# Moving the stacked copies of the keys from SyncE's queue to ScalarE's in a two-layer graph attention kernel

## The chip, the cores and the metric

One Trainium2 chip; the kernel runs on one of its cores. The metric is the device time of one launch in microseconds. Three runs of the kernel before took 1937.61 us (median; 1935.70 to 1940.65).

## The reference

The input `x` is 32 batches of 256 nodes by 384 features, `adj` is 32 sparse 256x256 matrices. Three layers follow each other, all in fp32; the outer two normalisations have no learned scale.

```python
def graph_layer(h, adj, wl, bl, ws, bs, wr, br, g, beta):          # twice: layers a and b
    a     = softmax(h @ h.T / sqrt(384), axis=-1)
    delta = a * adj
    attn  = delta / (delta.sum(-1, keepdims=True) + 1e-10)
    hl, hs, hr = h @ wl.T + bl, h @ ws.T + bs, h @ wr.T + br
    ctx = (attn * upper) @ hl + diag(attn)[:, None] * hs + (attn * lower) @ hr
    return relu(layernorm(ctx, 1e-12) * g + beta)

y   = layernorm(x + graph_layer_b(graph_layer_a(x)))
q, k, v = heads(y @ Wq + bq), heads(y @ Wk + bk), heads(y @ Wv + bv)   # 12 heads of 32: layer c
s   = where(adj > 0, q @ k.T / sqrt(32) + 0.1 * adj, -9e15)
out = layernorm(y + softmax(s) @ v)
```

## The kernel before

A batch is two row tiles of 128 nodes. Every fp32 operand of a large product is held as a rounded high part and a low rest, and each product is three matmuls (high x high, low x high, high x low). ScalarE (ACT) writes the high part out of PSUM, VectorE (DVE) subtracts it to get the low one.

The kernel is a software pipeline over batches: in pass `t`, layer a works on batch `t`, layer b on batch `t-1`, attention (layer c) on batch `t-2`, and the last normalisation on batch `t-3`. Within a pass each engine has a fixed list of steps, written out in `ORDER` (L46 to L77). A word `scores.8-1` is step `scores`, part 8, of the pass before (`-1`: it belongs to the batch that entered attention one pass ago). The five lists run beside each other and meet only at semaphores, so where a step stands in its engine's list decides what it is queued behind. There is no dynamic scheduling.

Names used below, for one batch in attention:

- `q.g`, `k.g` (g = 0 to 2): projection of 128 of the 384 query or key features, on TensorE (PE) into `bank_w`; ACT writes `qk_hi` (L666), DVE `qk_lo` (L863). `v.i` (i = 0, 1): the values; ACT writes them at L674, DVE the rest at L872.
- `q_stack.r`, `k_stack.r` (r = 0 to 3): the copies that this document is about. Heads r, r+4 and r+8 lie in the partitions 32r to 32r+31 of `qk_hi` and `qk_lo`. Three DMAs, one per slot, put high, low and high (for keys high, high, low) of these three heads under each other in 96 partitions of `q_st` and `k_st` (32 partitions x 3 heads x 256 fp32, 96 KB each), so that one matmul over 96 rows gives the whole three-term product of a head. So a batch has 12 DMAs for the queries and 12 for the keys.
- `scores.n` (n = 0 to 11, heads in the order of `HEADS`, L41): two matmuls `bank_s<-k_st,q_st`. They wait for the query and key copies of their group r; `scores.0` needs group 0, `scores.3` group 1, `scores.6` group 2, `scores.9` group 3. DVE adds the mask and takes the minimum (L883), ACT takes the exponential (L682).
- `weights.n`: ACT (L690) and DVE (L888) write the two fp16 halves of the weights, then SyncE (SP) issues a DMA transpose of them into `pT` (L355). `attend.n` multiplies `pT` with the values into `bank_o`.
- `b_proj.0` to `b_proj.5`: the three projections of layer b for two row tiles, alternating between the two PSUM banks `bank_w0` and `bank_w1`. `b_proj.2` writes bank 0 again, and so waits until ACT (L611) and then DVE (L790) have read `b_proj.0` out of it; `b_proj.3` waits likewise for `b_proj.1`.

Both DMA transposes and the 24 copies, and the loads of `x` and `adj`, are issued by SP in its own order. ACT issues one store per batch (L658). The lines of the lists that matter here: after the three key projections PE does `k.2 turn_h.1 v.0 turn_h.2 attend.10-1 v.1 turn_x.0 attend.11-1 b_scores.0 turn_x.1 scores.0 b_proj.0 scores.1 b_proj.1 b_proj.2 b_proj.3`, and ACT does `turn_x.0 v.0 v.1 scores.0 b_proj.0 turn_x.1 weights.0 scores.1 b_proj.1`.

Of the kernel before, what the change touches and what calls it, by code (L numbers as in the profile page):

```python
# [21 lines left out]
F32 = mybir.dt.float32  # L22
# [11 lines left out]
SLOTS = 3  # L34
# [22 lines left out]
        turn_h.0 k.1 weights.11-1 turn_h.1 k.2 turn_h.2 turn_x.0 v.0 v.1 scores.0 b_proj.0 turn_x.1 weights.0  # L57
        scores.1 b_proj.1 b_scores.0 weights.1 b_proj.2 b_turn.0 turn_x.2 b_proj.3 scores.2 b_proj.4 weights.2
        c_norm.0 scores.3 b_proj.5 weights.3 a_scores.0 c_apply.0 c_store.0 scores.4 weights.4 b_norm.0
        a_proj.0 b_apply.0 scores.5 weights.5 a_proj.1 scores.6 weights.6 a_turn.0 a_proj.2 scores.7 a_proj.3  # L60
        b_norm2.0""",
# [12 lines left out]
        weights.5-1 k_stack.3-1 q_stack.3-1 weights.6-1 a_x.0 weights.7-1 c_adj.0 weights.8-1 weights.9-1  # L74
        weights.10-1 q_stack.0 weights.11-1 k_stack.0 k_stack.1 b_adj.0 weights.0 q_stack.1 k_stack.2 a_adj.0
        weights.1 b_x.0 weights.2 q_stack.2 weights.3 weights.4""",
# [35 lines left out]
def graph_attention_kernel(nc, x, adj, wl, ws, wr, bl, bs, br, ln_w, ln_b,  # L112
# [3 lines left out]
    NC = D // P  # L116
    HD = D // NH
    HPG = P // HD
# [9 lines left out]
    with ExitStack() as ctx:  # L128
# [42 lines left out]
        qk_hi = sb("qk_hi", [P, 2, NC, S], F32R)  # L171
        qk_lo = sb("qk_lo", [P, 2, NC, S], F32R)
        q_st = sb("q_st", [P, NH, S], F32R)
# [89 lines left out]
        def wait(eng, s, count):  # L263

            if count > 0:
                eng.wait_ge(s, count)
# [38 lines left out]
        def _(sp):  # L305
            def stack(t, side, r):

                c = t - 2
                if r == 0:
                    wait(sp, s_qk_lo, NC * (2 * c + side + 1))  # L310
                for slot in range(SLOTS):
                    part = (qk_hi, (qk_lo, qk_hi)[side], (qk_hi, qk_lo)[side])[slot]
                    sp.dma_start((q_st, k_st)[side][slot * HD:(slot + 1) * HD, r::HPG, :].bitcast(F32),  # L313
                                 part[r * HD:(r + 1) * HD, side, :, :].bitcast(F32)).then_inc(s_stack["qk"[side]][r], 16)
# [43 lines left out]
            def load(n):  # L358
# [9 lines left out]
                "q_stack": lambda t, r: stack(t, 0, r), "k_stack": lambda t, r: stack(t, 1, r),  # L368
# [183 lines left out]
        def _(act):  # L552
# [132 lines left out]
            def weights(t, k):  # L685
# [6 lines left out]

            steps = {
                "split": split, "turn_x": turn_x, "turn_h": turn_h, "turn_y": turn_y,
# [349 lines left out]
```

## Time and profile before

| | |
|---|---|
| median of three runs | 1937.61 us |
| profiled execution: its own time | 1934.71 us |
| profiled execution: span, first to last instruction | 1933.0 us |
| busy share PE / DVE / ACT / POOL | 91% / 80% / 65% / 34% |
| mean granted clock of TensorE | 0.976 of full speed |
| DMA queue of SP, of ACT: share of 16 engines' time | 57.2%, 2.1% |

The program has 36 passes, of which some 30 in the middle are full; the windows from 110 to 1850 us lie in these. Busy times of an engine add up its instructions; issuing a DMA is not counted as busy and stands in the rows as SPq (SyncE's queue) or ACTq (ScalarE's). In the timeline a row gives the start in us, the duration, the engine, the line, the operation and, in brackets, how long the engine had been idle and whose work it had been waiting for.

### The profile page before, as it was taken

To read this page: it belongs to the slowest core of one execution; us is meant where nothing else is said; L and a number is where in the kernel's file an instruction comes from. 1 tells how busy PE (TensorE), PEld (TensorE's weight loads), DVE (VectorE), ACT (ScalarE), POOL (GpSimd) and SP (SyncE) were. 2 spreads that over 40 slices of the span, in tenths; PEclk is the share of its full clock that TensorE was granted. 3 is DMA by queue.
4 is the path that set the end of the run, shared out by engine and by line. 5 is a ranking of instruction groups with operands and counts; after the bars stand their busy time and mean duration, and the time that the engine had idled before them with its cause. 6 is when DMAs were issued, how large, how long until landed. Compare 5 with 4: busy or idle time off the path is not lost.

```text
span 1933.0 us, 39870 instructions
## 1 busy us (share of the span) xinstructions
PE 1752.1 (91%) x13120; PEld 1639.3 (85%) x13120; DVE 1554.9 (80%) x5383; ACT 1260.2 (65%) x3036; POOL 650.5 (34%) x777
## 2 busy tenths in 40 slices
PE   4899999999999999999999999999999989999963
PEld 4798898889888888998888889888988989898852
DVE  4578888888888888887898788888888879888864
ACT  3466676766666766666676667666666767666643
POOL 0223333333343234333333334323433323333431
PEclk9899999999999999999999999999999999999975
DMA  4045566665665666566666566566656665656655
GB/s 150 28 108 129 129 129 146 127 146 122 137 131 122 142 133 138 124 130 127 140 133 141 120 136 132 119 142 135 141 120 132 135 130 126 144 124 130 120 117 109
DMA packets 550036, 247.65 MB, mean 128 GB/s; under 512 B 423100, under 2 KB 549832, under 8 KB 549832
## 3 DMA queue, kind: packets, MB, share of 16 engines
q1 hardware_dynamic: 538928, 231.91, 57.2%
q10 hardware_dynamic: 10904, 13.20, 2.1%
q8 instruction: 106, 1.74, 0.4%
q14 instruction: 98, 0.80, 0.1%
HBM read 56.25 MB, written 12.58 MB: 36 GB/s over the span
## 4 chain that ended last, share of the span: by engine, by line
PE 43%; DVE 21%; DMA 21%; SPq 7%; ACT 4%; issue 3%; ACTq 0%; POOL 0%; DVEq 0%; POOLq 0%
PE bank_w L383 25%; DMA pT<-halves 20%; PE bank_u L383 5%; PE bank_o L383 4%; DVE bank_s L883 4%; SPq L313 4%; DVE halves L888 4%; PE bank_m L383 3%; PE bank_s L383 3%; SPq L355 2%; DVE mixed L801 2%; DVE pairs L764 1%; ACT halves L690 1%; DVE qk_lo L863 1%; DVE result L899 1%
## 5 line engine op out<-in xcount | busy, mean ns | idle before, releaser
L682 ACT ACTIVATE bank_s<-bank_s,hmin 128x256 f32<-128x256 f32 x768 | 312.1, 450 | 146.5 <-DVE hmin L883 131.4
L883 DVE CUSTOM_DVE_ANT_0 bank_s<-bank_s,bias_adj 128x256 f32<-128x256 f32 x768 | 310.7, 446 | 98.5 <-PE bank_s L383 94.4
L690 ACT ACTIVATE halves<-bank_s 128x512 f16<-128x512 f32 x384 | 229.4, 597 | 118.1 <-DMA pT<-halves 116.3
L888 DVE TENSOR_TENSOR halves<-bank_s,halves 128x512 f16<-128x512 f32 x384 | 261.5, 681 | 30.5 <-ACT halves L690 29.6
L383 PE MATMUL bank_o<-v_parts,pT 128*128 128x99 bf16 (+1 forms) x3072 | 181.4, 204 | 59.2 <-DMA pT<-halves 39.6
L383 PEld LDWEIGHTS bank_o<-v_parts,pT 128*128 128x128 f16 x3072 | 140.7, 99 | 101.0 <-DMA pT<-halves 56.7
L383 PE MATMUL bank_w<-w_graph0h,hT_ach 128*128 128x384 f32 x576 | 206.7, 359 | 6.7 <-DVE w_graph0l L743 5.4
L383 PE MATMUL bank_s<-k_st,q_st 96*128 96x256 f32 x768 | 178.2, 314 | 25.7 <-DVE halves L888 14.2
L383 PE MATMUL bank_w<-w_graph1h,hT_bh 128*128 128x384 f32 x576 | 197.7, 343 | 0.0
L383 PE MATMUL bank_w<-w_graph0l,hT_ach 128*128 128x384 f32 x576 | 195.4, 339 | 0.0
L383 PE MATMUL bank_w<-w_graph0h,hT_acl 128*128 128x384 f32 x576 | 195.3, 339 | 0.0
L383 PE MATMUL bank_w<-w_graph1l,hT_bh 128*128 128x384 f32 x576 | 195.2, 339 | 0.0
L383 PE MATMUL bank_w<-w_graph1h,hT_bl 128*128 128x384 f32 x576 | 194.7, 338 | 0.0
L966 POOL TENSOR_SCALAR v_rest<-adj_in 128x512 f32<-128x512 f32 x32 | 61.7, 1928 | 374.7 <-issue 374.7
L383 PE MATMUL bank_w<-hT_ach,w_qkvh 128*128 128x256 f32 x576 | 172.0, 299 | 4.0 <-DVE hT_acl L755 1.2
L984 POOL TENSOR_TENSOR normed<-normed,g_row 128x384 f32<-128x384 f32 x64 | 63.1, 1006 | 330.8 <-ACT normed L631 330.8
L383 PE MATMUL bank_w<-hT_acl,w_qkvh 128*128 128x256 f32 x576 | 162.4, 282 | 0.0
L383 PE MATMUL bank_w<-hT_ach,w_qkvl 128*128 128x256 f32 x576 | 162.4, 282 | 0.0
L955 POOL TENSOR_SCALAR_AFFINE_SELECT uph<-attTh 128x256 fp32r<-128x256 f32 x64 | 26.3, 410 | 392.0 <-DVE attTl L795 392.0
L383 PEld LDWEIGHTS bank_s<-k_st,q_st 96*128 96x128 f32 x768 | 123.6, 195 | 37.4 <-DVE halves L888 18.4
L790 DVE TENSOR_TENSOR hlrl<-bank_w,hlrh 128x384 fp32r<-128x384 f32 x256 | 138.2, 549 | 10.7 <-ACT hlrh L611 8.1
L611 ACT ACTIVATE hlrh<-bank_w 128x384 fp32r<-128x384 f32 x256 | 125.0, 488 | 24.1 <-PE bank_w L383 19.5
(177 smaller groups left out, 5319.8 us busy)
## 6 DMA issues: line engine op xcount, KB each, us to landing
x_in<-in_x SPq DMA_DIRECT2D x64, 384.0 KB, 3.6
adj_in<-in_adj SPq DMA_DIRECT2D x96, 256.0 KB, 3.2
q_st<-qk_hi SPq DMA_DIRECT2D x256, 96.0 KB, 2.3
k_st<-qk_hi SPq DMA_DIRECT2D x256, 96.0 KB, 2.2
q_st<-qk_lo SPq DMA_DIRECT2D x128, 96.0 KB, 2.2
k_st<-qk_lo SPq DMA_DIRECT2D x128, 96.0 KB, 2.2
out<-result ACTq DMA_DIRECT2D x32, 384.0 KB, 3.7
pT<-halves SPq DMA_TRANSPOSE x384, 3.1
```

Source lines behind the costliest of these rows:

```text
L313: sp.dma_start((q_st, k_st)[side][slot * HD:(slot + 1) * HD, r::HPG, :].bitcast(F32), part[r * HD:(r + 1) * HD, side, :, :].bitcast(F32)). ...
L355: sp.dma_start_transpose(pT[:, k % 2, :, :], halves[:, k % 2, :, :, :].rearrange("p i a s -> p (i a s)")).then_inc(s_pt[k % 2], 16)
L383: return nc.tensor.matmul(dst, lhsT, rhs, start=start, stop=stop)
L611: nc.scalar.activation(hlr[0][:, i, m // 2, :], bank_w[i][:, 0:D], ACT.Copy).then_inc(s_proj_hi, 1)
L682: nc.scalar.activation(bank[:, i * S:(i + 1) * S], bank[:, i * S:(i + 1) * S], ACT.Exp, bias=hmin[:, i, k:k + 1], scale=-1.0).then_inc(s_p ...
L690: nc.scalar.activation(halves[:, k % 2, :, 0, :], bank_s[k % 2][:, :].rearrange("p (i s) -> p i s", i=NT), ACT.Copy).then_inc(s_pt_hi, 1)
L790: ve.tensor_tensor(hlr[1][:, i, m // 2, :], bank_w[i][:, 0:D], hlr[0][:, i, m // 2, :], ALU.subtract).then_inc(s_proj_rd, 1)
L801: ve.tensor_tensor(mixed[:, i, :], bank_m[:, 0:D], self_part[:, i, :], ALU.add).then_inc(s_mix_rd, 1)
L883: ve.tensor_tensor_reduce(bank_s[k % 2][:, i * S:(i + 1) * S], bank_s[k % 2][:, i * S:(i + 1) * S], bias_adj[:, i, :], -SCALE, BIG, ALU.ad ...
L888: ve.tensor_tensor(halves[:, k % 2, :, 1, :], bank_s[k % 2][:, :].rearrange("p (i s) -> p i s", i=NT), halves[:, k % 2, :, 0, :], ALU.subtract
L966: gp.tensor_scalar(neg_adj[:, :, :], adj_in[:, :, :], 0.0, MASKED / SCALE, ALU.is_le, ALU.mult).then_inc(s_pool, 1)
L984: gp.tensor_tensor(normed[:, i, :], normed[:, i, :], g2_row[:, :], ALU.mult).then_inc(s_affine_mid, 1)
```

## The change

The twelve key copies of a batch are no longer issued by SP but by ACT, in a step `k_stack` with the same four parts, which stands in ACT's list behind `v.1` and ahead of `scores.0`. All four groups stand there together; on SP they were spread over the pass (group 0 and 1 behind `weights.11-1`, group 2 behind `q_stack.1`, group 3 in the next pass behind `weights.5-1`). The wait for the low parts of the keys (`s_qk_lo`) moves with them. The query copies stay where they are in SP's list. Source, destination, size and semaphores of each copy are the same, and no computing instruction changes or moves.

```diff
--- before.py
+++ after.py
@@ ORDER
     "act": """
...
-        turn_h.0 k.1 weights.11-1 turn_h.1 k.2 turn_h.2 turn_x.0 v.0 v.1 scores.0 b_proj.0 turn_x.1 weights.0
...
+        turn_h.0 k.1 weights.11-1 turn_h.1 k.2 turn_h.2 turn_x.0 v.0 v.1 k_stack.0 k_stack.1 k_stack.2
+        k_stack.3 scores.0 b_proj.0 turn_x.1 weights.0 scores.1 b_proj.1 b_scores.0 weights.1 b_proj.2
...
     "sp": """
-        weights.5-1 k_stack.3-1 q_stack.3-1 weights.6-1 a_x.0 weights.7-1 c_adj.0 weights.8-1 weights.9-1
-        weights.10-1 q_stack.0 weights.11-1 k_stack.0 k_stack.1 b_adj.0 weights.0 q_stack.1 k_stack.2 a_adj.0
-        weights.1 b_x.0 weights.2 q_stack.2 weights.3 weights.4""",
+        weights.5-1 q_stack.3-1 weights.6-1 a_x.0 weights.7-1 c_adj.0 weights.8-1 weights.9-1 weights.10-1
+        q_stack.0 weights.11-1 b_adj.0 weights.0 q_stack.1 a_adj.0 weights.1 b_x.0 weights.2 q_stack.2
+        weights.3 weights.4""",
@@ ScalarE
+            def k_stack(t, r):
+
+                c = t - 2
+                if r == 0:
+                    act.wait_ge(s_qk_lo, NC * (2 * c + 2))
+                for slot in range(SLOTS):
+                    act.dma_start(k_st[slot * HD:(slot + 1) * HD, r::HPG, :].bitcast(F32),
+                                 (qk_hi, qk_hi, qk_lo)[slot][r * HD:(r + 1) * HD, 1, :, :].bitcast(F32)
+                                 ).then_inc(s_stack["k"][r], 16)
```

ScalarE's queue in the kernel before, around the two activations of the values' projection (L674); L682 and L690 are `scores` and `weights`, L611 is `b_proj`, L578 is `turn_x`.

```order
L578 ACTIVATE hT_ach<-bank_t 128x256
L674 ACTIVATE v_parts<-bank_w 128x12x32 x2
L682 ACTIVATE bank_s<-bank_s,hmin 128x256 x2
L611 ACTIVATE hlrh<-bank_w 128x384
L578 ACTIVATE hT_ach<-bank_t 128x256
L690 ACTIVATE halves<-bank_s 128x2x256
```

`scores.0` stands right behind the values there. The same place of the same queue in the changed kernel (L699 are the key copies):

```order
L578 ACTIVATE hT_ach<-bank_t 128x256
L674 ACTIVATE v_parts<-bank_w 128x12x32 x2
L699 DMA k_st<-qk_hi 32x3x256 x2
L699 DMA k_st<-qk_lo 32x3x256
L699 DMA k_st<-qk_hi 32x3x256 x2
L699 DMA k_st<-qk_lo 32x3x256
L699 DMA k_st<-qk_hi 32x3x256 x2
L699 DMA k_st<-qk_lo 32x3x256
L699 DMA k_st<-qk_hi 32x3x256 x2
L699 DMA k_st<-qk_lo 32x3x256
L682 ACTIVATE bank_s<-bank_s,hmin 128x256 x2
L611 ACTIVATE hlrh<-bank_w 128x384
```

Twelve DMAs now stand between the values and `scores.0`; what was there keeps its order behind them.

SyncE's queue in the kernel before, from the transpose of `weights.11-1` on (L313 are the copies, L334 and L348 the loads of `adj`, L355 the transposes).

```order
L355 DMA_TRANSPOSE pT<-halves 128x8x128
L313 DMA k_st<-qk_hi 32x3x256 x2
L313 DMA k_st<-qk_lo 32x3x256
L313 DMA k_st<-qk_hi 32x3x256 x2
L313 DMA k_st<-qk_lo 32x3x256
L334 DMA adj_in<-in_adj 128x2x256
L355 DMA_TRANSPOSE pT<-halves 128x8x128
L313 DMA q_st<-qk_hi 32x3x256
L313 DMA q_st<-qk_lo 32x3x256
L313 DMA q_st<-qk_hi 32x3x256
L313 DMA k_st<-qk_hi 32x3x256 x2
L313 DMA k_st<-qk_lo 32x3x256
```

Six key copies lie between the first two transposes and three behind the query copies. The same place of the queue in the changed kernel, where the copies are at L312:

```order
L355 DMA_TRANSPOSE pT<-halves 128x8x128
L334 DMA adj_in<-in_adj 128x2x256
L355 DMA_TRANSPOSE pT<-halves 128x8x128
L312 DMA q_st<-qk_hi 32x3x256
L312 DMA q_st<-qk_lo 32x3x256
L312 DMA q_st<-qk_hi 32x3x256
L348 DMA adj_in<-in_adj 128x2x256
```

Six DMAs are gone between the transposes of `weights.11-1` and `weights.0`, and three between those of `weights.0` and `weights.1`.

## Rows read from the trace of the kernel before

**Rows 1.** page, part 1 and part 4 by line.

```profile
PE 1752.1 (91%) x13120; PEld 1639.3 (85%) x13120; DVE 1554.9 (80%) x5383; ACT 1260.2 (65%) x3036; POOL 650.5 (34%) x777
...
PE bank_w L383 25%; DMA pT<-halves 20%; PE bank_u L383 5%; PE bank_o L383 4%; DVE bank_s L883 4%; SPq L313 4%; DVE halves L888 4%; PE bank_m L383 3%; PE bank_s L383 3%; SPq L355 2%; DVE mixed L801 2%; DVE pairs L764 1%; ACT halves L690 1%; DVE qk_lo L863 1%; DVE result L899 1%
```

**Rows 2.** waits over the span: who waited for whom, us, times, longest.

```profile
PE bank_o L383 <- DMA pT<-halves: 39.6, 46, 2.1
...
PE bank_m L383 <- DVE mixed L801: 23.2, 33, 1.6
```

**Rows 3.** windows: stretch, us, busy of PE PEld DVE ACT POOL, clock, DMA share, GB/s.

```profile
110.00:1850.00 1740.00, 1639.14 (x12434) 1539.09 (x12433) 1457.23 (x5079) 1181.51 (x2855) 614.67 (x732) 1.00 0.62 132
1574.60:1578.00 3.40, 3.40 (x13) 3.40 (x13) 1.81 (x7) 0.88 (x3) 0.00 (x0) 0.52 0.11 25
```

**Rows 4.** chain of waits, 897 to 1012: start us, us, what.

```profile
900.23 4.82 DMA pT<-halves
...
957.82 3.09 DMA pT<-halves
...
972.99 0.54 DVE halves L888
...
975.07 3.58 DMA pT<-halves
```

**Rows 5.** timeline of SyncE's queue: first and last of five key copies.

```profile
959.14 1.24 SPq L313 DMA_DIRECT2D k_st<-qk_hi  x2
...
962.37 0.61 SPq L313 DMA_DIRECT2D k_st<-qk_lo  x1
```

**Rows 6.** timeline of PE: starts of the steps around the change.

```profile
905.11 0.47 PE L383 MATMUL bank_o<-v_parts,pT 128*128 128x99 bf16 x8 [1.60 <-DMA pT<-halves]
...
963.64 0.48 PE L383 MATMUL bank_s<-k_st,q_st 96*128 96x256 f32 x2
...
967.72 0.34 PE L383 MATMUL bank_w<-w_graph1h,hT_bh 128*128 128x384 f32 x1
...
969.48 0.34 PE L383 MATMUL bank_w<-w_graph1h,hT_bh 128*128 128x384 f32 x1
...
1574.04 0.48 PE L383 MATMUL bank_o<-v_parts,pT 128*128 128x99 bf16 x8 [1.90 <-DMA pT<-halves]
```

**Rows 7.** timeline of ACT: the values, scores.0, b_proj.0, b_proj.1.

```profile
961.53 0.88 ACT L674 ACTIVATE v_parts<-bank_w 128x384 bf16<-128x384 f32 x2 [0.35 <-PE bank_o L383]
965.06 0.81 ACT L682 ACTIVATE bank_s<-bank_s,hmin 128x256 f32<-128x256 f32 x2 [2.65 <-DVE hmin L883]
965.92 0.49 ACT L611 ACTIVATE hlrh<-bank_w 128x384 fp32r<-128x384 f32 x1
...
967.92 0.49 ACT L611 ACTIVATE hlrh<-bank_w 128x384 fp32r<-128x384 f32 x1
```

**Rows 8.** timeline of DVE: b_proj.0 read out of bank 0.

```profile
966.89 0.55 DVE L790 TENSOR_TENSOR hlrl<-bank_w,hlrh 128x384 fp32r<-128x384 f32 x1
```

**Rows 9.** one line each, all its DMAs: duration ns min/median/max; landing of L313.

```profile
L313 SPq DMA_DIRECT2D k_st<-qk_hi x256: 585/600/1788, 105.8 to 1902.6; - x128
...
DMA to landing us min/median/max: 2.2/2.3/4.9
...
L658 ACTq DMA_DIRECT2D out<-result x32: 378/392/412, 184.9 to 1930.1; - x32
...
L320 SPq DMA_DIRECT2D adj_in<-in_adj x32: 378/581/841, 84.6 to 1858.6; - x32
```

**Rows 10.** timeline of ACT's start: table load and first DMA.

```profile
0.79 1.28 ACT L553 ACT_TABLE_LOAD   x1 [0.79 <-PEq L1028]
0.82 0.84 ACTq L558 DMA_DIRECT2D self_part<-in_L_gnn_bl  x2
```

**Rows 11.** timeline: the store on ACT's queue beside SyncE's copies.

```profile
983.13 0.38 ACTq L658 DMA_DIRECT2D out<-result  x1
...
983.26 0.61 SPq L313 DMA_DIRECT2D q_st<-qk_hi  x1
```

More of the change, by code:

```diff
@@ L56 @@
         turn_y.2-1 weights.9-1 scores.10-1 q.0 h_norm.0 q.1 weights.10-1 q.2 h_apply.0 k.0 scores.11-1
-        turn_h.0 k.1 weights.11-1 turn_h.1 k.2 turn_h.2 turn_x.0 v.0 v.1 scores.0 b_proj.0 turn_x.1 weights.0
[L58 to L61, printed above, removed]
+        turn_h.0 k.1 weights.11-1 turn_h.1 k.2 turn_h.2 turn_x.0 v.0 v.1 k_stack.0 k_stack.1 k_stack.2
+        k_stack.3 scores.0 b_proj.0 turn_x.1 weights.0 scores.1 b_proj.1 b_scores.0 weights.1 b_proj.2
+        b_turn.0 turn_x.2 b_proj.3 scores.2 b_proj.4 weights.2 c_norm.0 scores.3 b_proj.5 weights.3 a_scores.0
+        c_apply.0 c_store.0 scores.4 weights.4 b_norm.0 a_proj.0 b_apply.0 scores.5 weights.5 a_proj.1
+        scores.6 weights.6 a_turn.0 a_proj.2 scores.7 a_proj.3 b_norm2.0""",
     "dve": """
@@ L305, in _, with stack @@
         def _(sp):
-            def stack(t, side, r):
+            def stack(t, r):
                 c = t - 2
                 if r == 0:
-                    wait(sp, s_qk_lo, NC * (2 * c + side + 1))
+                    wait(sp, s_qk_lo, NC * (2 * c + 1))
                 for slot in range(SLOTS):
-                    part = (qk_hi, (qk_lo, qk_hi)[side], (qk_hi, qk_lo)[side])[slot]
-                    sp.dma_start((q_st, k_st)[side][slot * HD:(slot + 1) * HD, r::HPG, :].bitcast(F32),
-                                 part[r * HD:(r + 1) * HD, side, :, :].bitcast(F32)).then_inc(s_stack["qk"[side]][r], 16)
+                    sp.dma_start(q_st[slot * HD:(slot + 1) * HD, r::HPG, :].bitcast(F32),
+                                 (qk_hi, qk_lo, qk_hi)[slot][r * HD:(r + 1) * HD, 0, :, :].bitcast(F32)
+                                 ).then_inc(s_stack["q"][r], 16)
             def c_adj(t, _k):
@@ L367, in _ @@
                 "c_adj": c_adj, "a_x": a_x, "b_adj": b_adj, "b_x": b_x, "a_adj": a_adj, "weights": weights,
-                "q_stack": lambda t, r: stack(t, 0, r), "k_stack": lambda t, r: stack(t, 1, r),
+                "q_stack": stack,
             }
@@ L691, in weights @@
                                      ACT.Copy).then_inc(s_pt_hi, 1)
+            def k_stack(t, r):
[6 more added lines that the diff above has]
+                                 ).then_inc(s_stack["k"][r], 16)
             steps = {
+                "k_stack": k_stack,
                 "split": split, "turn_x": turn_x, "turn_h": turn_h, "turn_y": turn_y,
```

## The prediction

> **What bounds the kernel now.** I read the page first: TensorE is busy 91% of the span [rows 1]. The window over the full passes says how much is left: 1639.14 busy of 1740 us, so 100.9 us idle [rows 3]. The transposes of `weights.11` are issued at 900.23 and 957.82 [rows 4], so a pass is 57.6 us, the window holds 30.2 of them, and PE idles 3.3 us in each. So PE's own order of work is nearly the bound. Whatever makes PE wait is paid in full, and relieving another engine can give back 3.3 us per pass at most.
>
> The chain of waits shows SP's queue on the path all the same: 4% of the span are SPq L313, the stacked copies, and 20% are transposes on their way [rows 1]. The waits of PE name what is at the end of these: 39.6 us for the transposes of `pT` and 23.2 us for `mixed` from DVE [rows 2]. Then I followed one pass (957 to 985 us) engine by engine, and an issue on each queue by its line.
>
> **What the change takes away.** SP loses 12 issues per batch. Five of them span 959.14 to 962.37, 0.646 us apiece with the gap between them [rows 5], so SP is freed of 7.8 us per pass. What was late because of them:
> - The transpose of `weights.11-1` has six key copies issued right behind it. It takes 4.82 us to land in the pass at 900, 3.09 us in the next one [rows 4]; PE then waits 1.60 us at attend.11 [rows 6]. Ten of the 30 middle passes have this wait (1.50 to 1.65 us). With the copies issued later it should go: 0.5 us per pass.
> - The transpose of `weights.1` stands behind `q_stack.1`, `k_stack.2` and a load. Its data is ready at 973.53 (972.99 + 0.54), it is issued at 975.07 [rows 4]: 1.5 us of SP's making, less than the 1.9 us of three copies. It goes through ACT and DVE to `mixed`, for which PE waits 23.2 us in all, 0.7 us per pass [rows 2]. I count all of that.
> - `k_stack.3` ahead of `weights.6`: PE's other waits for `pT` are 39.6 - 10 x 1.6 = 24 us, 0.75 us per batch; I count 0.2, since most of them end at transposes that stand behind no key copy.
>
> Sum 1.4 us per batch; bounds 0 and 3.3.
>
> **What it adds, on ACT.** What does an issue of this shape cost there? The trace has none, only neighbours [rows 9]. On SP a key copy never took under 585 ns, median 600. A load of `adj` on SP took 378 ns at best, and ACT's store of `out` takes 378 to 412. Where both queues issue a plain wide DMA on its own they pay the same, so I take SP's price of the copy, 0.646 us with its gap, from the same kind of DMA; the low bound is the store's 0.38 + 0.05 = 0.43.
>
> When does the burst begin? ACT's first DMA was issued at 0.82 while its table load ran from 0.79 to 2.07 [rows 10]: an issue doesn't wait for the activation ahead to finish. The key parts are long written. So it begins when the second values' activation has been sent off, about 962.0 (two activations from 961.53 to 962.41 [rows 7]). Then, on the pass at 961:
> - Third copy of group 0 issued at 962.0 + 2 x 0.646 = 963.3, landed 2.3 us later [rows 9]: 965.6. `scores.0` began on PE at 963.64 [rows 6]: **PE waits 2.0 us**.
> - From `scores.0` to `b_proj.2` PE needs 967.72 - 963.64 = 4.08 us [rows 6], so it is at `b_proj.2` at 969.7.
> - ACT is through the burst at 962.0 + 12 x 0.646 = 969.75. Behind it are queued `scores.0`, `b_proj.0`, and everything of ACT's pass. `b_proj.0` starts 0.86 us later and takes 0.49 [rows 7]: 971.1. DVE needs 0.55 [rows 8], PE may write bank 0 again at 971.65: **a second wait of 1.95 us**, 3.9 late in all.
> - `b_proj.1` is read by ACT 2.0 us behind `b_proj.0` with no idle time between [rows 7]: 972.6 to 973.1, DVE to 973.65. PE is there at 971.65 + 1.76 = 973.4 [rows 6]. Another 0.25: **4.2 us late** against 969.48.
>
> After this ACT, DVE and PE are late by about the same and the pass goes on as before. ACT's 65% doesn't help: its slack lies elsewhere in the pass. `q_stack.1` moves too, behind `weights.0` which ACT and DVE now finish at about 972.6; its copies land near 977.5, PE wants them for `scores.3` about 978. No term, but little room.
>
> The Trainium skill (DMA: Bandwidth & Descriptors, "Issuing engines are not separate DMA queues") says that issuing from several engines saves only the sequencer's time, which is "usually small relative to the DMA itself". The rows agree that a copy's 2.3 us don't shrink, but 0.6 us of issue is a quarter of them, and twelve in a row are not small. By that rule there would be little to gain and little to lose; by the rows the loss is 4.2.
>
> **Sum.** 4.2 - 1.4 = 2.8 us per batch, x 32 = 90 us. In the last batches nothing of other layers covers the burst: 5 us. For the clock (below) 5 us. Together 100 us on the profiled execution's own 1934.7 (span 1933.0): 2035. The median of the runs is 2.9 us above that execution: **2038 us**. Its own range: 2.0 to 4.2 us per batch, 2002 to 2082.
>
> **Rivals.**
> 1. *The issues on ACT cost what its store costs, 0.43 us.* The burst ends at 967.15, group 0 lands at 965.15: PE waits 1.5. ACT passes `b_proj.0` to DVE at 968.5, DVE is done at 969.05, PE comes at 969.2: no second wait. 1.5 against 1.4 gained: 1938 +- 10. If the gains on SP are larger than I counted, with 3.3 us of idle time at most to recover, the kernel is faster: this is the other side, decided at the issue price of about 0.43 us and below; at 2.5 us recovered it is 1905. For it: the store's 392 ns. Against it: SP's own wide loads alone also take 378 ns and its copies never do.
> 2. *The clock falls.* At 1574.04 PE had waited 1.90 us [rows 6], and for the 3.4 us that followed the granted clock was 0.52, that is 1.2 GHz for nearly all of it [rows 3]; the waits of 1.60 were followed by none. The change brings two waits of about 2 us close together. Half the pace for 3.4 us costs 1.7 us; behind the first wait it is covered by the second, behind the second it isn't. 32 x 1.7 = 54: 2090, more if it stays low.
> 3. *The queue relief gives back all of PE's idle time but the burst costs as computed.* 4.2 - 3.3 = 0.9 per batch: 1970. Against it: waits for `bank_t`, and between DVE and PE, have nothing to do with SP.
> 4. *The change does nothing*, because ACT's queue hides the issues beside its activations, as its first DMA lay beside the table load. But `scores.0` stands behind all twelve in one queue, and ACT idles only 2.65 us there [rows 7]. 1938.
>
> By the same skill (Perfetto Trace Analysis, "DMA Instruction — HWDGE (DVE, Sync)") the descriptor generator is locked for exclusive use, and a profiled issue includes the wait for it, so SP's issues would stretch the burst; with its one load in that stretch 0.6 us more per batch, 2057. The rows don't bear it out: the store's 0.38 us on ACT began at 983.13, SP's copy at 983.26 took its usual 0.61 [rows 11].
>
> **Chances.** As forecast 0.66; rival 1 as no change 0.05 and as faster 0.05; rival 2 0.12; rival 3 0.10; rival 4 0.02. Under about 0.3% (6 us) a measurement can't tell from no change. So faster 0.05, same 0.07, slower 0.88. The range for 8 in 10 leaves out the lower cases of rival 1 and 4 and the far end of rival 2: 1955 to 2095.
>
> **What would show it.** In the profile after: twelve ACTq rows behind L674, of 0.6 us each (0.4 would be rival 1); PE idle 2 us ahead of the first `bank_s` of a batch, with the copies of `k_st` as releaser, and again 2 us ahead of `b_proj.2`, with DVE L790; attend.11 without its 1.6 us; the transposes of `weights.1` within 0.3 us of their data; PE's busy time unchanged unless the clock falls. The forecast is wrong if the issues are short, if the burst begins only when ACT has time, or if PE's idle time per pass stays near 3.3 us.

## The result, and the profile after

The changed kernel takes 2054.35 us (median of four runs, 2050.11 to 2065.21) against 1938.86 us for the kernel before: a ratio of 1.0606, 95% interval 1.0562 to 1.0650. It is slower by 116 us; forecast were 100 us (2038 us, range 1955 to 2095). The profiled execution took 2054.59 us, its span is 2052.9 us.

The page of the changed kernel, part 1 and part 4 by line, answers to [rows 1]:

```profile
PE 1791.9 (87%) x13120; PEld 1666.2 (81%) x13120; DVE 1586.7 (77%) x5383; ACT 1253.9 (61%) x3036; POOL 650.1 (32%) x777
...
PE bank_w L383 21%; DMA pT<-halves 10%; ACTq L699 8%; PE bank_m L383 5%; DVE bank_s L894 5%; DVE halves L899 4%; PE bank_o L383 4%; DVE hlrl L801 3%; PE bank_u L383 3%; PE bank_s L383 3%; SPq L312 2%; DVE mixed L812 1%; DVE attTl L806 1%; ACT bank_s L682 1%; DVE stats_y L860 1%
```

The transposes in flight fell from 20% of the chain to 10%, SP's copies from 4% to 2%, and the key copies on ACT's queue (L699) are now 8% of it. PE's waits over the span, answering to [rows 2]:

```profile
PE bank_s L383 <- issue: 52.6, 31, 4.4
PE bank_w L383 <- DVE hlrl L801: 52.0, 26, 3.2
PE bank_o L383 <- DMA pT<-halves: 25.8, 23, 2.0
...
PE bank_m L383 <- DVE mixed L812: 7.9, 32, 1.0
```

The first two rows are new: PE ahead of `scores.0` (the profile names no releaser there, "issue") and ahead of `b_proj.2`, 104.6 us together, 3.3 per batch. The last two fell by 29.1 us, 0.9 per batch.

To see what a pass costs I take the same 29 passes of each kernel, from one attend.11 to another. Columns: stretch, us, busy of PE, PEld, DVE, ACT, POOL, granted clock, DMA share, GB/s. The kernel before, then the changed one:

```profile
163.50:1819.90 1656.40, 1565.34 (x11889) 1470.00 (x11888) 1390.83 (x4843) 1127.35 (x2726) 585.03 (x696) 1.00 0.62 132
```

```profile
167.80:1932.20 1764.40, 1601.94 (x11889) 1494.52 (x11889) 1420.44 (x4843) 1121.32 (x2726) 584.69 (x696) 0.98 0.59 124
```

Divided by 29, a pass took 57.12 us and takes 60.84: 3.72 us more, 108 of the 120 us between the two profiled executions (2052.9 - 1933.0 by span). PE's idle time grew from 91.1 to 162.5 us (2.46 per pass) and its busy time by 36.6 us (1.26 per pass) with the same number of matmuls: most of that part is a slower clock (16 stretches, 61 us together, at a granted clock of 0.50, against one of 3.4 us before). POOL is as busy as before. DVE runs the same 4843 instructions and is busy 29.6 us longer, nearly all of it in one small instruction (`pairs<-pairs`, L776, which takes up to 1341 ns, 389 before).

One pass of the changed kernel on ACT: start, duration, engine, operation, idle time before. It answers to [rows 7].

```profile
965.29 0.50 ACT L674 ACTIVATE v_parts<-bank_w 128x384 bf16<-128x384 f32 x1 [1.78 <-PE bank_o L383]
965.35 0.63 ACTq L699 DMA_DIRECT2D k_st<-qk_hi  x1
...
965.69 0.49 ACT L674 ACTIVATE v_parts<-bank_w 128x384 bf16<-128x384 f32 x1
...
972.57 0.62 ACTq L699 DMA_DIRECT2D k_st<-qk_lo  x1
973.24 0.81 ACT L682 ACTIVATE bank_s<-bank_s,hmin 128x256 f32<-128x256 f32 x2 [7.06 <-DVE hmin L894]
973.97 0.49 ACT L611 ACTIVATE hlrh<-bank_w 128x384 fp32r<-128x384 f32 x1
```

The same pass on PE, in order attend.11, `scores.0`, `b_proj.2`, and the DVE instruction that lets `b_proj.2` start (answers to [rows 6] and [rows 8]):

```profile
964.72 0.47 PE L383 MATMUL bank_o<-v_parts,pT 128*128 128x99 bf16 x8 [1.63 <-DMA pT<-halves]
...
969.64 0.47 PE L383 MATMUL bank_s<-k_st,q_st 96*128 96x256 f32 x2 [1.98 <-issue]
...
975.11 0.44 PE L383 MATMUL bank_w<-w_graph1h,hT_bh 128*128 128x384 f32 x1 [1.22 <-DVE hlrl L801]
```

```profile
974.49 0.56 DVE L801 TENSOR_TENSOR hlrl<-bank_w,hlrh 128x384 fp32r<-128x384 f32 x1 [0.97 <-ACT hlrh L611]
```

Read them together. The burst begins at 965.35 while an activation runs, takes 7.22 us for its first eleven copies (0.656 apiece), and ACT computes nothing from 966.18 to 973.24. PE waits 1.98 us for group 0's copies (the third is issued at 966.66 and lands 2.9 us later), then 1.22 us for a bank that ACT had no time to read. Both waits stand where they were foreseen. The usual pass divides them otherwise: over the 30 middle passes the medians are 1.36 us ahead of `scores.0` and 1.85 ahead of `b_proj.2`. In none of the 32 bursts does SP issue anything meanwhile.

All key copies of the changed kernel by line, answering to [rows 9] (ns, min/median/max):

```profile
L699 ACTq DMA_DIRECT2D k_st<-qk_hi x256: 592/624/1996, 109.9 to 1999.9; - x128
...
DMA to landing us min/median/max: 2.2/2.2/4.2
```

### The profile page after: what moved, and what is told of

Its sections match the earlier page's. It is cut to its first block, busy times and chain, and to the rows that moved or that the text cites. A ratio compares the mean times of both kernels' runs of the same rounds, so it can differ in the third digit from the quotient of the medians.

```text
span 2052.9 us, 39870 instructions
## 1 busy us (share of the span) xinstructions
PE 1791.9 (87%) x13120; PEld 1666.2 (81%) x13120; DVE 1586.7 (77%) x5383; ACT 1253.9 (61%) x3036; POOL 650.1 (32%) x777
## 3 DMA queue, kind: packets, MB, share of 16 engines
q8 instruction: 106, 1.74, 0.4%
## 4 chain that ended last, share of the span: by engine, by line
PE 39%; DVE 27%; DMA 11%; ACTq 8%; ACT 6%; issue 5%; SPq 3%; POOL 0%; DVEq 0%; POOLq 0%
PE bank_w L383 21%; DMA pT<-halves 10%; ACTq L699 8%; PE bank_m L383 5%; DVE bank_s L894 5%; DVE halves L899 4%; PE bank_o L383 4%; DVE hlrl L801 3%; PE bank_u L383 3%; PE bank_s L383 3%; SPq L312 2%; DVE mixed L812 1%; DVE attTl L806 1%; ACT bank_s L682 1%; DVE stats_y L860 1%
## 5 line engine op out<-in xcount | busy, mean ns | idle before, releaser
L682 ACT ACTIVATE bank_s<-bank_s,hmin 128x256 f32<-128x256 f32 x768 | 313.6, 453 | 283.8 <-DVE hmin L894 199.4
L690 ACT ACTIVATE halves<-bank_s 128x512 f16<-128x512 f32 x384 | 231.6, 603 | 84.9 <-DMA pT<-halves 81.4
L383 PE MATMUL bank_w<-w_graph1h,hT_bh 128*128 128x384 f32 x576 | 212.4, 369 | 51.9 <-DVE hlrl L801 51.7
L383 PE MATMUL bank_s<-k_st,q_st 96*128 96x256 f32 x768 | 179.3, 316 | 75.6 <-issue 52.6
L383 PE MATMUL bank_o<-v_parts,pT 128*128 128x99 bf16 (+1 forms) x3072 | 180.7, 204 | 48.1 <-DMA pT<-halves 25.8
L383 PE MATMUL bank_w<-w_graph1l,hT_bh 128*128 128x384 f32 x576 | 204.9, 356 | 0.0
L383 PE MATMUL bank_w<-w_graph1h,hT_bl 128*128 128x384 f32 x576 | 204.4, 355 | 0.0
L383 PEld LDWEIGHTS bank_w<-w_graph1h,hT_bh 128*128 128x128 f32 x576 | 115.7, 201 | 63.4 <-DVE hlrl L801 62.9
```

The source lines that it names most:

```text
L383: return nc.tensor.matmul(dst, lhsT, rhs, start=start, stop=stop)
L682: nc.scalar.activation(bank[:, i * S:(i + 1) * S], bank[:, i * S:(i + 1) * S], ACT.Exp, bias=hmin[:, i, k:k + 1], scale=-1.0).then_inc(s_p ...
L690: nc.scalar.activation(halves[:, k % 2, :, 0, :], bank_s[k % 2][:, :].rearrange("p (i s) -> p i s", i=NT), ACT.Copy).then_inc(s_pt_hi, 1)
```

## The experiments

Per-pass numbers below are the profiled stretch of the same 29 passes, divided by 29; before is 57.12, the changed kernel 60.84. Ratios are against the kernel before, run beside it. In the step lists `K0` to `K3` stand for `k_stack.0` to `k_stack.3`.

### 1. No key copies at all

This gives the ceiling of what SP's relief is worth. The keys of the first batch are copied, later ones never, so all later scores use those keys.

```diff
             def stack(t, side, r):
+                if side == 1 and c > 0:
+                    return
-                    pe.wait_ge(s_stack["k"][h], STACKED * (s + 1))
+                    pe.wait_ge(s_stack["k"][h], STACKED)
```

> The kernel before, with the twelve key copies issued for the first batch alone; the later batches use the first one's stacked keys, so 31 x 12 copies are left out and nothing takes their place. It gives the whole worth of SP's relief with no cost on ACT. Theory (relief is small, the burst on ACT is what costs): PE's wait for `mixed` shrinks from 23 us to about 8 as in the changed kernel, the ten waits of 1.6 us at attend.11 stay, 1910 to 1922 us. Rival (SP's queue was a real bound, and the changed kernel lost more than 3.7 us per batch on ACT): 1880 or less. Second rival (relief is worth nothing): 1938.

Measured 1902.82 us, ratio 0.9828 (0.9803 to 0.9853). Window and waits:

```profile
166.10:1788.10 1622.00, 1560.08 (x11890) 1468.35 (x11890) 1388.74 (x4843) 1126.22 (x2726) 585.64 (x696) 1.00 0.54 114
```

```profile
PE bank_o L385 <- DMA pT<-halves: 23.7, 20, 2.1
```

This is below the 1910 to 1922 us expected. At 55.93 us per pass, taking the copies away altogether is worth 1.19 us per pass (33 us or 1.04 per batch by the medians). The two waits, for transposes and for `mixed` (9.4 us here), fall to about what the changed kernel has (25.8 and 7.9), so the change did collect the relief. Rival 3 (3.3 us of relief) is out: PE's other idle time stays when no key copy is issued.

### 2. The burst alone, with SP as before

The keys are stacked by SP as in the kernel before, and ACT issues twelve copies into an unused tile where the changed kernel has its own (224 of 256 columns each, since no more memory was free).

```diff
-        ... v.0 v.1 K0 K1 K2 K3 scores.0 ...            (ACT; SP without key copies)
+        ... v.0 v.1 spare.0 spare.1 spare.2 spare.3 scores.0 ...   (ACT; SP as before)
```

> The kernel before with all its copies on SP, and beside them twelve more copies of the keys per batch (32 partitions x 3 heads x 224 of 256 columns) from ACT's queue behind v.1 into a spare buffer that nobody reads. It has ACT's burst without the late landing of group 0 and without SP's relief. Theory (ACT's queue is held for 7.8 us): no wait ahead of the first scores, one wait of about 3.9 us ahead of b_proj.2 on DVE L790, 3.9 to 4.2 us per batch with no relief, plus what the clock takes: 2070 to 2110 us. Rival (the loss is the late landing of the keys): 1940 to 1960. Rival (the loss is traffic of two queues on the same engines): landing times of SP's copies grow above 2.3 us.

Measured 2138.28 us, ratio 1.1044 (1.1011 to 1.1076).

```profile
172.30:2011.80 1839.50, 1628.79 (x11890) 1524.12 (x11888) 1393.12 (x4843) 1121.34 (x2726) 584.21 (x696) 0.96 0.63 135
```

```profile
PE bank_w L385 <- DVE hlrl L806: 140.2, 32, 6.6
PE bank_o L385 <- DMA pT<-halves: 41.1, 47, 2.1
```

This is 28 us above the range expected (2070 to 2110). A pass takes 63.43 us, 6.31 more than before. Without the late landing PE doesn't wait at `scores.0`, but the whole delay comes at `b_proj.2`: 4.4 us each time, the 4.2 us of the sum in one piece. PE's busy time is 63 us above before (37 in the changed kernel), so a single long wait costs more clock than two short ones. The waits for transposes stay as in [rows 2]: their relief in experiment 1 and in the change is that of SP's queue. The wait for `mixed` doesn't show that by itself, since it falls to 8.6 us here although SP issues every key copy: I read this as a late and slow PE hiding it. What SP's relief does to it is seen in experiment 1, and at full clock, where it is 9.1 us with SP relieved (experiment 3) and 20.6 without (experiment 6). The copies on SP still land in 2.2 to 2.3 us in the median beside the spare ones, so traffic isn't the loss.

### 3. The changed kernel with PE kept busy in both waits

```diff
+                if j == 2 and n % 2 == 1 and n >= 3:      # ahead of b_proj.2
+                    pe.wait_ge(s_mix_rd, 2 * n)
+                    fill(bank_m, 12)                      # 12 matmuls, results unused
+                if k == 0 and t <= NB:                    # ahead of scores.0
+                    wait(pe, s_pt_lo, NH * s + k - 1)
+                    fill(bank_s[0], 14)
```

> The changed kernel, with TensorE given work that nobody reads in its two waits: 14 matmuls of 256 columns ahead of the wait for the copies of scores.0, 12 ahead of the wait of b_proj.2. Theory (36.6 us of PE's longer busy time in 29 passes are the 1.2 GHz stretches that follow the two waits): these stretches go from the middle of the trace and the time falls by 25 to 38 us, to 2016 to 2030. Rival (the stretches are covered by the second wait and cost nothing, or the busy time is longer for another reason): 2054, or above it where the added work is longer than a wait.

Measured 2045.29 us, ratio 1.0568 (1.0541 to 1.0595), only 9 us below the changed kernel where 25 to 38 were expected.

```profile
168.30:1918.40 1750.10, 1663.34 (x12643) 1562.90 (x12644) 1417.51 (x4843) 1120.38 (x2726) 585.25 (x696) 1.00 0.59 125
```

The granted clock is back at 1.00 and a pass takes 60.35 us, 0.5 less. That isn't yet what the slow clock cost, since the added matmuls cost time of their own: 27 of the 29 passes here have no slow stretch and take 60.12 us on average, while 14 passes of the changed kernel have none either and take 59.30. The other 15 passes of the changed kernel have 4.1 us at 1.2 GHz each on average and take 62.28, with two waits that are as long together (3.36 against 3.30). Two of its passes, whose two waits are the same (1.35 and 1.85 us; 1.36 and 1.83), the second with 3.4 us at 1.2 GHz behind `b_proj.2`:

```profile
1023.72:1082.35 58.63, 54.15 (x410) 50.67 (x411) 49.19 (x167) 38.33 (x93) 20.17 (x24) 1.00 0.62 128
1203.36:1263.64 60.28, 55.52 (x411) 52.23 (x411) 49.30 (x167) 38.51 (x94) 20.15 (x24) 0.97 0.59 126
```

That is 1.65 us for one slow stretch. All passes with such waits say the same: 12 without a slow stretch average 59.09 us, 5 with one 60.72. Over all passes the clock so costs between 0.8 us (1.63 x 15 / 29) and 1.5 us each (60.84 - 59.30); the upper figure contains longer waits in some of the slow passes. Of the 16 slow stretches ten follow the wait ahead of `b_proj.2`, five the one ahead of `scores.0`, one another. The changed kernel's pass at 904 is one of the five; its wait ahead of `scores.0`, and the window behind it:

```profile
904.96 0.77 PE L383 MATMUL bank_s<-k_st,q_st 96*128 96x256 f32 x2 [2.79 <-issue]
```

```profile
904.60:908.00 3.40, 3.04 (x10) 3.07 (x11) 2.05 (x7) 0.00 (x0) 2.59 (x2) 0.50 0.60 146
908.00:911.40 3.40, 3.40 (x13) 3.40 (x13) 2.01 (x7) 2.69 (x7) 0.00 (x0) 0.52 0.35 86
```

For some 6.8 us PE runs at 1.2 GHz (0.50 and 0.52), and in that pass there is no wait ahead of `b_proj.2`: there the slow matmuls fill time in which PE would have waited for ACT anyway, and only what exceeds the second wait is lost.

### 4 and 5. Half a burst, and the burst without group 0

One kernel leaves groups 2 and 3 on SP, the other leaves group 0 there.

```diff
 half:        ACT ... v.0 v.1 K0 K1 scores.0 ...      SP: K2, K3 as before
 no group 0:  ACT ... v.0 v.1 K1 K2 K3 scores.0 ...   SP: K0 behind weights.11-1
```

> Groups 0 and 1 of the key copies on ACT behind v.1, groups 2 and 3 with SP at their old places. ACT is held 3.9 us in place of 7.8. Theory (two separate waits, the first from the late landing of group 0, the second from the length of the burst): the wait ahead of the first scores stays at 1.6 to 2.0 us per batch, the one ahead of b_proj.2 is gone, SP's relief is near zero because groups 2 and 3 still stand ahead of weights.1 and weights.6; 1990 to 2012 us. Rival (one cost in proportion to the issues on ACT): half of the loss, 1995, but with both waits still there and half as long.

> Group 0 stays with SP at its old place, groups 1 to 3 on ACT behind v.1: nine issues, 5.8 us. Theory: no wait ahead of the first scores; ACT reaches scores.0 at 2.8 us behind its old time and PE waits 2 us ahead of b_proj.2; SP's relief of about 1 us per batch is there; 1970 to 1998 us. Rival (the late landing of group 0 is the whole loss): 1905 to 1915.

Half: 2028.58 us (expected 1990 to 2012), ratio 1.0480 (1.0455 to 1.0505), 60.07 per pass. Without group 0: 1983.67 us (expected 1970 to 1998), ratio 1.0252 (1.0235 to 1.0269), 58.33 per pass. PE's waits, the half first:

```profile
PE bank_s L383 <- issue: 52.3, 31, 4.3
PE bank_o L383 <- DMA pT<-halves: 41.3, 49, 2.1
PE bank_m L383 <- DVE mixed L812: 27.4, 33, 1.6
...
PE bank_w L383 <- DVE hlrl L801: 16.3, 23, 0.8
```

```profile
PE bank_w L383 <- DVE hlrl L801: 54.1, 32, 2.6
PE bank_o L383 <- DMA pT<-halves: 24.0, 20, 2.1
...
PE bank_m L383 <- DVE mixed L812: 6.8, 29, 0.7
```

These two take the delay apart. The first wait depends on where group 0 is and not on the length of the burst: 52.3 us with six copies as with twelve, gone when group 0 stays on SP. The second depends on the length. With six copies it all but goes (16.3 us), yet the kernel is nearly as slow as the changed one, because it has none of the relief: the waits for transposes (41.3) and for `mixed` (27.4) are those of before. The relief belongs to groups 2 and 3, the first wait to group 0. The rival that late landing is the whole loss (1905 to 1915 without group 0) is out.

### 6. The spare burst with PE kept busy

Experiment 2 with 34 matmuls ahead of `b_proj.2` in each pass.

```diff
+                if j == 2 and n % 2 == 1 and n >= 3:
+                    pe.wait_ge(s_mix_rd, 2 * n)
+                    fill(bank_m, 34)
```

> The spare burst (all copies on SP, twelve unused ones from ACT behind v.1) with 34 matmuls of 256 columns, read by nobody, on TensorE ahead of the wait of b_proj.2. Theory (31 stretches at 1.2 GHz, 157 us of them, follow the 4.4 us waits, and with no second wait to cover them they cost about 2 us each): the stretches go and the time falls from 2138 to 2065 to 2085 us although TensorE has more to do. Rival (the granted clock is a sign and not a cost here): 2138 or more.

Measured 2111.21 us, ratio 1.0910 (1.0894 to 1.0926), 62.44 per pass at a clock of 1.00. The sign is as expected, 27 us below experiment 2, but 53 to 73 us had been expected. A fill of 34 matmuls takes about 4.2 us, while the waits it covers vary around 4.4, so part of it is overshoot. The clock costs something behind one long wait, 1 us per pass net of what the added matmuls cost; most of the 6.3 us of experiment 2 is plain waiting.

### 7. The copies spread over ACT's idle stretches

Group 0 behind the last `turn_h`, ahead of the wait for `turn_x`; group 1 behind `v.1`; group 2 behind `b_proj.5`; group 3 behind `weights.3`. No key copies on SP.

```diff
-        ... turn_h.2 turn_x.0 v.0 v.1 K0 K1 K2 K3 scores.0 ... b_proj.5 weights.3 a_scores.0 ...
+        ... turn_h.2 K0 turn_x.0 v.0 v.1 K1 scores.0 ... b_proj.5 K2 weights.3 K3 a_scores.0 ...
```

> All twelve key copies on ACT as in the changed kernel, but in four places where ACT was idle before: group 0 behind turn_h.2, group 1 behind v.1, group 2 behind b_proj.5, group 3 behind weights.3. Theory (the queue is not the fault, the place is): both waits of the changed kernel are gone, the relief of SP is left, 1910 to 1930 us, under the kernel before. Rival (copies from ACT's queue cost what they cost wherever they stand, 7.8 us of a queue that is 65% busy): 1990 or more.

Measured 1916.98 us, ratio 0.9897 (0.9870 to 0.9924): faster than both kernels, and within the 1910 to 1930 us expected.

```profile
163.54:1792.36 1628.82, 1557.94 (x11889) 1468.88 (x11889) 1392.34 (x4843) 1126.17 (x2726) 585.32 (x696) 1.00 0.62 134
```

```profile
PE bank_o L383 <- DMA pT<-halves: 26.0, 21, 2.1
PE bank_m L383 <- DVE mixed L812: 24.0, 33, 1.1
```

A pass takes 56.17 us, 0.95 below before and 0.24 above having no copies at all. The profiled execution was one of the two fastest of six (1910.44 us); by the medians the gain is 19 us, 0.6 per batch. Both waits of the burst are gone, no slow clock is left in the middle, the waits for transposes have fallen as in experiment 1. Only the wait for `mixed` stayed. On ACT, groups 2 and 3 lie just ahead of layer a's exponential, which leads to `mixed`:

```profile
914.47 1.91 ACTq L699 DMA_DIRECT2D k_st<-qk_lo  x1
916.42 0.45 ACT L596 ACTIVATE bank_u<-bank_u,pairs 128x256 f32<-128x256 f32 x1 [2.65 <-issue]
```

(This copy is a stretched one, with a transfer of instructions beside it; the five ahead of it take 0.59 to 0.62 us.) In this kernel both queues issue at the same time, here at the transpose of `weights.11`, a copy of group 0 and a load of `adj`:

```profile
948.52 1.30 SPq L355 DMA_TRANSPOSE pT<-halves  x1
...
949.65 0.63 ACTq L699 DMA_DIRECT2D k_st<-qk_hi  x1
...
949.87 0.58 SPq L334 DMA_DIRECT2D adj_in<-in_adj  x1
```

Neither is stretched by the other. Of the 384 key copies 65 begin while an issue of SP is under way; they take 617 ns in the median and 819 at most.

### 8 to 10. Three attempts to get the rest

```diff
 8:  ACT ... turn_h.2 K0 turn_x.0 v.0 v.1 K1 scores.0 ... weights.1 K2 b_proj.2 ... weights.3 K3 a_scores.0 ...
 9:  ACT ... K0, K1 as in 7 ... b_proj.5 K2 weights.3 ... and of K3 one copy each behind scores.4, scores.5, scores.6
10:  as 9, but K0 and K1 on SP where before has them
```

> All twelve on ACT, group 0 behind turn_h.2, group 1 behind v.1 as in the first spread kernel, group 2 behind weights.1 and group 3 behind weights.3, so that no two groups stand together ahead of layer a's exponentials. Theory (in the first spread kernel PE still waits 24 us for `mixed` because groups 2 and 3 hold ACT there; each group in an idle stretch of its own frees that): 1903 to 1912 us, near the 1902.8 of the kernel without key copies. Rival (it is SP's transposes and not ACT that this wait comes from): 1917 as in the first spread kernel.

> Groups 0 and 1 lie as in the kernel that came out at 0.990 of the kernel before (group 0 behind the last turn_h, group 1 behind the second values' activation). Of group 2 three copies stay behind b_proj.5, where the trace of before has ScalarE waiting 2.11 us for a transpose ahead of weights.3. Group 3 is cut into single copies, one behind each of the exps of scores.4, scores.5 and scores.6 (0.62 us each, beside an activation that is running), so that nothing but weights.3 stands between group 2 and layer a's exp. Theory (what held the 0.990 kernel back was group 3 ahead of layer a's exp: TensorE's waits on the addition into mixed stayed at 24.0 us in 33, where the kernel without key copies has 9.4 in 30): these fall to 9 to 14 us, the waits for the transposes stay at about 26 us, time 1897 to 1910 us, below the 1917 us. Rival (it was group 2, or any issue between scores.4 and scores.7 holds ScalarE's later steps up): the addition's waits stay above 20 us, or waits for weights or for a_proj come in their place, and the time is 1915 to 1930.

> Only groups 2 and 3 go from SP to ScalarE, placed as in the kernel beside it (group 2 behind b_proj.5, group 3 in single copies behind the exps of scores.4 to scores.6); groups 0 and 1 stay on SP where before has them. Theory (SP's relief comes from groups 2 and 3, which stand ahead of transposes that TensorE or ScalarE waits for; groups 0 and 1 cost SP nothing, since with those two alone on ScalarE the waits were as before: transposes 41.3 us, addition 27.4): same time as the kernel beside it within 5 us, 1897 to 1912 us. Rival (groups 0 and 1 on SP delay the next transposes as well, which the kernel with those alone on ScalarE could not show since the burst hid it): the waits for the transposes stay above 33 us and the time is 8 to 20 us above the kernel beside it.

All three missed their ranges (1903 to 1912, 1897 to 1910, 1897 to 1912). Number 8: 1929.47 us, ratio 0.9965 (0.9949 to 0.9981), 56.84 per pass. Number 9: 1947.06 us, ratio 1.0059 (1.0030 to 1.0088), 57.39 per pass. Number 10: 1947.23 us, ratio 1.0046 (1.0028 to 1.0064), 57.52 per pass. Two of PE's waits in 9:

```profile
PE bank_o L384 <- DMA pT<-halves: 36.5, 42, 2.0
...
PE bank_w L384 <- ACT self_part L607: 22.7, 24, 1.2
```

In 8 the wait for `mixed` is nearly gone (3.1 us), but PE's scores now wait 20.1 us in 29 for query copies that SP issues at the time of group 2. In 9 the wait for `mixed` stayed (23.5 us in 34) without group 3 ahead of the exponential. Number 8 has group 3 there and differs from experiment 7 by group 2 alone, so it is group 2 behind `b_proj.5` that keeps this wait, unless the new wait of 8 hides it; and group 3 in single copies brought a new wait for `self_part`, which ACT writes later in the same stretch, and gave the relief of the transposes back (36.5 us). I read this as the price of single 0.6 us copies in a stretch where ACT is the engine waited for; no run moves them alone. Numbers 9 and 10 agree within 0.2 us: in this order of steps groups 0 and 1 may stand on either queue.

### 11 and 12. Moving the instruction transfers

Section "why" tells what these are about: a 1.6 us wait at attend.11 in every third pass that the change left in place. 22 matmuls (two instructions each), once, while the pipeline fills, in the kernel before (11) and in that of experiment 7 (12).

```diff
+                if j == 2 and n == 3:
+                    pe.wait_ge(s_mix_rd, 2 * n)
+                    fill(bank_m, 22)
```

> The kernel before, with 22 matmuls more on TensorE, once, in the filling of the pipeline (two instructions each, results unused; about 3 us). Nothing else differs in the passes behind. What is disputed is the wait of 1.6 us at attend.11 in every third pass: of the 30 middle passes of before, ten have it and in these ten a 16 KB transfer of the instruction queue falls into the flight of that transpose; twenty have neither. Ten such transfers come in three passes, so they lie some 85 instructions of TensorE apart if the three passes are laid over each other, and 44 instructions more ahead of them move all of them by half of that spacing. Theory (the transfer delays the transpose): at attend.11 the ten waits of 1.6 us go, save where another transfer lands in the same place; if none comes elsewhere 16 us less in all and 3 us for the matmuls, 1924 us; 1920 to 1932. Rival (the transfer is no cause, the six key copies behind the transpose or the pass itself are): ten waits of 1.6 us as before, 1937 to 1944 us.

> The kernel of the best time so far (key copies on ScalarE in its idle stretches, 0.990 of before, 1917 us; ten waits of 1.5 to 1.85 us at attend.11) with the same 22 matmuls on TensorE in the filling of the pipeline. Theory (the instruction transfer delays the transpose): the ten waits go, 17 us less and 3 us for the matmuls, about 1903 us; 1898 to 1912. Rival (no cause): 1917 to 1923 us with the ten waits in place.

Number 11: 1930.06 us, ratio 0.9967 (0.9948 to 0.9986). None of the 30 middle passes has the wait of 1.5 us and more at attend.11 (the longest is 1.04 us), where ten had it. Two of the 30 transposes still have a transfer in their flight, which takes them to 3.7 and 3.9 us. A pass took 56.61 us (1641.7 us for 29), 0.51 less, in its profiled execution, which was also its fastest; the median gained 5 us of the 11 expected. Why less than the profiled execution, one trace doesn't tell. In it both waits of [rows 2] fell, from 39.6 and 23.2 us, and another grew from 9.8:

```profile
PE bank_o L383 <- DMA pT<-halves: 27.7, 36, 2.1
PE bank_m L383 <- DVE mixed L808: 18.7, 32, 1.6
PE bank_s L383 <- DMA q_st<-qk_hi: 17.2, 17, 4.0
```

Number 12: 1946.36 us, ratio 1.0065 (1.0044 to 1.0086), 29 us above the kernel of experiment 7 where 14 less were expected. The ten waits are there, 1.7 to 2.4 us, and in nine of them no instruction transfer lies in the flight of that transpose. In the pass at 913 it lies beside the transpose before it instead (from 905.17 on), and that one holds SP's queue 2.09 us instead of 1.23. So SP issues the next one 0.9 us later than usual and ACT's first key copy comes 0.25 us behind it, where 1.1 us is usual (L706 are the key copies):

```profile
904.62 2.09 SPq L355 DMA_TRANSPOSE pT<-halves  x1
...
908.78 1.30 SPq L355 DMA_TRANSPOSE pT<-halves  x1
...
909.03 0.66 ACTq L706 DMA_DIRECT2D k_st<-qk_hi  x1
```

The transpose of 908.78, that of `weights.11`, is in flight for 4.52 us. So there are two ways to a late transpose: an instruction transfer in its flight, or copies of the other queue that start right behind it. The traces of 7, 8, 9 and 12 separate the second cleanly. Of their 120 middle transposes of `weights.11`, 89 have no transfer in their flight. In 15 of these (four in 8, two in 9, nine in 12) ACT's first key copy starts within 0.62 us of the transpose, and all 15 take 4.15 us or more; in the other 74 it starts 0.67 us behind or later, and none takes over 3.3. Number 8 also puts group 2 beside the transpose of `weights.0`, and all 31 of these in the middle then take 3.9 us or more, 4.5 in the median, against 3.1 before. So the instruction transfers can be moved, and where they fall is worth up to 1.7%.

## Why the prediction held, point by point

- **Price of an issue on ACT: 0.646 us.** Measured 0.656 apiece with the gap, 624 ns in the median. Rival 1 (0.43) is out: the same queue issues its store in 0.38 us, and SP's price for this copy is 0.60, so here the price goes with the shape of the copy and not with the engine. By the lock rule of the Trainium skill (Perfetto Trace Analysis, "DMA Instruction — HWDGE (DVE, Sync)") the copies would have been stretched where SP issues too, which gave 2057 us. The result lies close to that figure, but not by that road: SP issues nothing during any of the bursts, and where both queues do issue at once, in experiment 7, the 65 copies concerned keep their price (617 ns in the median). Of the changed kernel's 384 key copies 12 take over 0.7 us, and ten of these have an instruction transfer beside them; of the other 372 five have.
- **Start of the burst.** I let it begin when the second values' activation is sent off, 0.47 us behind the first's start. It begins 0.06 us behind the first's start (965.35 against 965.29).
- **First wait, 2.0 us.** 1.98 in the pass shown, but 52.6 us over the span or 1.6 per batch. The place is right, the size a fifth too large.
- **Second wait, 1.95 us, and 0.25 more.** 1.22 in the pass shown, 52.0 us or 1.6 per batch, and none at `b_proj.3`. This step was too large as well. In the pass shown the bank was free 9.76 us after the values' start (974.49 + 0.56 - 965.29), where I had 10.12, and PE was there after 8.60 (975.11 - 1.22 - 965.29), where I had 8.17. Sum of waits 3.3 per batch instead of 4.2.
- **Relief of SP, 1.4 us.** Experiment 1 gives 1.19 for all there is, and the waits of the changed kernel show it collected. The size was nearly right and its parts were not. attend.11's 0.5 us did not go: the pass above still has 1.63. `mixed` gave 0.5 of its 0.7, and the waits for other transposes, which I put at 0.2, gave 0.4 (39.6 - 25.8 over 32).
- **Clock, 5 us in all.** PE's busy time grew by 36.6 us. By the changed kernel's own passes (experiment 3) it costs 0.8 to 1.5 us per pass, 24 to 45 us in 29 passes. This is the term that was most wrong, too small by about 20 us or more. Rival 2 named the mechanism and its price (1.7 us behind the second wait, 1.65 in the pair of passes shown) but charged it to every pass; 15 of 29 have it.
- **Sum.** 2.8 idle per batch forecast, 2.46 per pass measured; the clock makes 3.72 of it. In the passes without a slow stretch the change costs 2.2 us (59.30 - 57.12). Overstated waits and an understated clock stand against each other, so the mechanism held, but that 100 us came so near 116 is partly luck.

**The wait at attend.11.** I read the 4.82 us of that transpose as the doing of six key copies behind it. They are gone from there, and it still takes as long. What differs is another queue. DMA activity while that transpose is in flight: the kernel before at 900.2 (it waits), the kernel before at 957.8 to 961.0 (it doesn't; q1 is the only queue there), the changed kernel at 959.8 (it waits, with no key copies behind it). Rows: queue with packets, MB, share; transpose with its landing in us.

```profile
q8 instruction: 1, 0.02, 1.3%
...
pT<-halves SPq DMA_TRANSPOSE x1, 4.8
```

```profile
q1 hardware_dynamic: 1361, 0.54, 83.1%
...
pT<-halves SPq DMA_TRANSPOSE x1, 3.1
```

```profile
q8 instruction: 1, 0.02, 1.5%
...
pT<-halves SPq DMA_TRANSPOSE x1, 4.8
```

The kernel before, the changed one, and those of experiments 1 and 7 have, of the 30 middle passes, ten waits above 1.2 us each and a q8 transfer in the flight of exactly these ten transposes, and none in the other twenty. The kernels of 8 and 9 have four and two such waits more without a transfer, which are the ones with ACT's copies right behind the transpose (experiment 12). Experiment 11 moves the transfers and the waits go, which shows the cause for the kernel before. Comparing the two passes of [rows 4] by the copies on SP alone could not have told this, since both passes have the same copies.

## What to carry to other kernels

A DMA issue is an instruction of the engine that makes it. Moving it to an engine with 65% load is free only where that engine waits at that place of its list, so lay the issues into its idle stretches one by one, by the timeline, and keep those whose landing is awaited first out of any burst: the same twelve copies were worth +6.1% in one block and -1.0% spread. Read a relief from a run that leaves the work out before you count it, and when the same transpose is slow in some passes and not in others, compare these two passes over all queues, the instruction queue too.

## What the runs showed of the hardware that I had not expected

- A single 16 KB instruction transfer (106 of them in a launch, 1.74 MB) in the flight of the transpose of `weights.11` takes its landing from 3.1 to 4.8 us. It isn't so for every transpose: of all those between 110 and 1850 us of the kernel before, 89 have a transfer in their flight and 39 of them take over 4 us; of 277 without one, 11 do. Which overlaps hurt, stays open. The transfers follow TensorE's instruction stream: with 26 and 34 more matmuls per pass (experiments 3 and 6) there are 113 and 115 of them, and only five or six passes wait at attend.11. So adding instructions to TensorE can shift waits everywhere behind, which was worth -0.3% in one kernel and +1.7% in another (0.9897 to 1.0065) (experiment 12 against 7). Experiments 3 and 6 carry an unknown share of it.
- The same transpose on SyncE's queue took 4.15 us and more to land, not 3.1 to 3.3, where ScalarE's queue started a 96 KB copy within 0.62 us of it (15 of 15, against none of 74 where the copy started later; experiment 12). No run moves only these copies, so for this transpose the two go together in every case, which isn't yet a test; number 8 moved copies to another transpose, with the same result.
- DMA issues on ScalarE's queue start while an activation ahead of them is still running, but the next activation waits until the last of them is through.
- The two waits of the changed kernel, 3.3 us together, are followed by 3.4 or 6.8 us at 1.2 GHz in half of the passes (0.50 and 0.52 in the windows above). Such a stretch of 3.4 us costs about 1.65 us, less where PE would have waited again within that time.
